# A hybrid block kernel on one core: every place of its side work set anew in its tables

## What is computed

```python
x = x + attn(_layernorm(x), ...)          # RMS norm, 16 heads, causal softmax, output projection, plus its own normed input
x = x + ffn(_layernorm(x), ...)           # base matrix + shared and 6 routed low-rank matrices, top 2
x = x + ssm(_layernorm(x), ...)           # conv of 4 taps, silu, softplus, scan with 16 states, gate, projection
x = x + ffn(_layernorm(x), ...)           # the same ffn once more

def step(h, inputs):                      # the scan of ssm, over the 512 rows
    dt, bt, ct, xt_ = inputs
    decay = jnp.exp(A[None] * dt[:, :, None])
    inp = dt[:, :, None] * xt_[:, :, None] * bt[:, None, :]
    h = decay * h + inp
    y = jnp.einsum('bdn,bn->bd', h, ct)
    return (h, y)
```

## Time and profile before

| | us |
|---|---|
| median of 3 runs | 1929.06 (1927.0 to 1930.86) |
| the profiled execution, its own time | 1925.6 |
| its span, first to last instruction | 1923.0 |
| PE busy | 1713.8 (89%) |
| DVE busy | 1676.4 (87%) |
| ACT busy | 1400.5 (73%) |
| POOL busy | 1102.4 (57%) |
| mean granted TensorE clock | 0.977 of 2.4 GHz |

### The profile page before, as it was taken

One profiled execution on the slowest core, in us unless ns is written; L12 is line 12 of the kernel. 1 busy time (PEld: TensorE's weight loads), 2 busy tenths in 40 slices (PEclk: granted clock), 3 DMA queues, 4 the chain that ended last, 5 costly groups with the idle time before them and its releaser, 6 DMA issues.

```text
span 1923.0 us, 31523 instructions
## 1 busy us (share of the span) xinstructions
PE 1713.8 (89%) x9575; PEld 1006.4 (52%) x9620; DVE 1676.4 (87%) x3928; ACT 1400.5 (73%) x2724; POOL 1102.4 (57%) x903
## 2 busy tenths in 40 slices
PE   6989797999989898999999898999999898878875
PEld 2555454646455564646465565646455464535333
DVE  4654889999999999999999999999999899977892
ACT  3666768787887978787887878787877868675541
POOL 2000575667666676657667666657667566666330
PEclk9999899999999999999999999999999999999997
DMA  5312576978879797988879797988889687661110
GB/s 142 90 56 78 127 170 138 182 157 178 154 158 182 159 181 150 183 156 179 157 164 178 158 185 151 180 155 179 152 169 170 150 169 147 137 127 49 56 60 11
DMA packets 216331, 275.30 MB, mean 143 GB/s; under 512 B 37170, under 2 KB 129123, under 8 KB 216163
## 3 DMA queue, kind: packets, MB, share of 16 engines
q0 software_dynamic: 60480, 110.13, 34.8%
q1 hardware_dynamic: 155682, 163.17, 33.4%
HBM read 128.49 MB, written 34.08 MB: 85 GB/s over the span
## 4 chain that ended last, share of the span: by engine, by line
PE 48%; DVE 15%; ACT 12%; issue 9%; DMA 8%; POOL 7%; SPq 1%; another core or an unknown queue 0%; POOLq 0%; DVEq 0%; ACTq 0%
PE bank L423 9%; DVE hc L1275 7%; PE bank L542 5%; PE bank L625 4%; DMA y<-hc 4%; PE bank L487 4%; PE bank L509 4%; PE bank L642 4%; POOL inp L1449 3%; PE bank L434 3%; DVE bank L1131 2%; PE bank L417 2%; ACT pt L916 2%; DVE hc L1283 2%; PE bank L626 2%
## 5 line engine op out<-in xcount | busy, mean ns | idle before, releaser
L1449 POOL TENSOR_TENSOR inp<-u,b_all 128x1024 f32<-128x1024 f32 x240 | 572.8, 2386 | 361.0 <-issue 125.0
L1275 DVE TENSOR_TENSOR_SCAN hc<-dec,inp 128x1024 f32<-128x1024 f32 x256 | 585.8, 2288 | 39.7 <-POOL inp L1449 15.2
L1131 DVE CUSTOM_DVE_ANT_0 bank<-bank,mask_qk 128x512 f32<-128x512 f32 (+3 forms) x1024 | 479.4, 509 | 85.6 <-PE bank L487 85.0
L1459 POOL DMA_DIRECT2D y<-hc x420 | 368.5, 949 | 129.5 <-DMA y<-hc 64.9
L916 ACT ACTIVATE pt<-bank 128x512 f32<-128x512 f32 x640 | 380.1, 605 | 72.5 <-PE bank L525 49.3
L1032 ACT ACTIVATE dec<-dt,a_neg 128x511 f32<-128x511 f32 x512 | 339.6, 729 | 34.1 <-DVE hc L1275 34.0
L1283 DVE TENSOR_TENSOR hc<-hc,bank 128x1024 f32<-128x1024 f32 x242 | 294.0, 1215 | 14.2 <-PE bank L679 13.3
L487 PE MATMUL bank<-sk,sq 96*128 96x512 bf16 (+3 forms) x1024 | 250.3, 306 | 27.3 <-DVE mall L1131 16.7
L509 PE MATMUL bank<-sq,sk 98*128 98x512 bf16 (+3 forms) x1024 | 248.6, 304 | 27.0 <-ACT pt L916 23.4
L542 PE MATMUL bank<-pt,v_sb 128*32 128x512 f32 (+3 forms) x2048 | 180.5, 450 | 7.5 <-ACT pt L916 6.8
L487 PEld LDWEIGHTS bank<-sk,sq 96*128 96x128 bf16 x1024 | 95.3, 99 | 145.0 <-issue 54.8
(11 more groups left out here) (169 smaller groups left out, 2999.0 us busy)
## 6 DMA issues: line engine op xcount, KB each, us to landing
y<-hc POOLq DMA_DIRECT2D x420, 256.0 KB, 4.9
b_all<-b_kept SPq DMA_DIRECT2D x256, 256.0 KB, 3.7
qk_parts<-parts SPq DMA_DIRECT2D x96, 256.0 KB, 3.0
sq<-qk_parts SPq DMA_DIRECT2D x384, 64.0 KB, 3.7
sk<-qk_parts SPq DMA_DIRECT2D x384, 64.0 KB, 3.9
X<-in_x SPq DMA_DIRECT2D x16, 512.0 KB, 6.1
out<-X SPq DMA_DIRECT2D x16, 512.0 KB, 3.3
sq<-hlt SPq DMA_DIRECT2D x256, 2.0 KB
```

The lines of the kernel that those rows point to most:

```text
L1131: return V.tensor_tensor_reduce(src[:, o:o + n], src[:, o:o + n], mask_qk[:, T - n:T], 1.0, -3.0e38, ALU.add, ALU.max, out)
L1275: V.tensor_tensor_scan(h, d, v, 0.0, ALU.mult, ALU.add).then_inc(scan_done.sem, 1)
L1449: G.tensor_tensor(inp[:, n % 2, :, :], u[:, :, :], b_all[:, k % 3, None, :].to_broadcast([P, C, T]), ALU.mult).then_inc(inp_ready.sem, 1)
L1459: pool.dma_start(y[:, s % 2, c, :], hc[:, (NS * s + n) % HC, c, :], accum_op=ALU.add).then_inc(y_added[c].sem, 16)
```

## The change

All five tables, those of the kinds 1 to 3 and `BANK` get other numbers. No instruction is added or removed, no wait is added or removed, and no code outside the tables changes. After the change the tables take one line less, so every line number of the code behind them is lower by one: line 487 becomes 486, and so on.

```diff
-    PE_AT = {"res": (-32, -29), "xn": (-73, -72), "qk00": (-56, -51, -47), "qk01": (-47, -44, -43),
+    PE_AT = {"res": (-32, -29), "xn": (-73, -72), "qk00": (-56, -50, -49), "qk01": (-47, -44, -43),
...
-    BANK = {"res": (0, 0), "xn": (0, 1), "qk00": 0, "qk01": 1, "v": (1, 1), "qk10": 0, "qk11": 1, "ao": (0, 1),
+    BANK = {"res": (0, 0), "xn": (1, 0), "qk00": 0, "qk01": 1, "v": (1, 1), "qk10": 0, "qk11": 1, "ao": (0, 1),
...
-    POOL_AT = {"rsqrt_f": 89, "rsqrt_s": 122, "rsqrt_q": -113, "rsqrt_l": 234, "low": (110, 258),
+    POOL_AT = {"rsqrt_f": 83, "rsqrt_s": 123, "rsqrt_q": -113, "rsqrt_l": 234, "low": (110, 258),
```

More of the change, by code:

```diff
@@ L121, in hybrid_block @@
-    SP_AT = {"parts": (-40, -3), "load_x": -114, "store_b": 149, "store": 280, "stack": (-32, -32, -33),
-             "maxima": -6, "load_b": (150, 151, 156, 160, 168, 173, 185, 185, 190, 198, 199, 210, 211, 215, 224, 225)}
+              "scan": (160, 167, 169, 171, 177, 185, 192, 197, 201, 205, 211, 214, 218, 224, 229, 232),
+              "product": (168, 170, 171, 177, 182, 190, 195, 199, 203, 210, 212, 215, 222, 227, 229, 236)}
+    POOL_AT = {"rsqrt_f": 83, "rsqrt_s": 123, "rsqrt_q": -113, "rsqrt_l": 234, "low": (110, 258),
+               "inputs": (147, 149, 152, 152, 157, 165, 175, 183, 191, 199, 206, 211, 214, 218, 220, 222),
+               "add": (160, 152, 159, 174, 176, 182, 187, 191, 200, 208, 212, 214, 219, 221, 223, 228)}
@@ L123, in hybrid_block @@
+    SP_AT = {"parts": (-40, -3), "load_x": -114, "store_b": 149, "store": 282, "stack": (-31, -31, -32),
+             "maxima": -10,
+             "load_b": (150, 152, 157, 160, 164, 172, 180, 187, 192, 198, 200, 209, 210, 213, 225, 225)}
     OWN = {
         1: {
[7 rows of a table removed]
-                   "sum": (136, 151, 160, 164, 165, 173, 174, 186, 189, 196, 202, 202, 218, 219, 225, 225)},
-            "ACT": {"res": (-51, -42), "square_f": 92, "square_s": 127, "norm_f": 98, "norm_q": -106, "norm_l": 254,
[4 rows of a table removed]
-                   "decays": (154, 157, 163, 167, 168, 180, 182, 190, 197, 202, 205, 210, 215, 219, 225, 228)},
@@ L139, in hybrid_block @@
[L139 to L145, removed]
@@ new lines, in hybrid_block @@
+            "ACT": {"res": (-53, -45), "square_f": 92, "square_s": 127, "norm_f": 98, "norm_q": -100, "exp0": 108,
[4 rows of a table added]
+                   "decays": (155, 155, 164, 166, 168, 180, 182, 189, 196, 204, 205, 211, 213, 217, 221, 226)},
+            "DVE": {"gated": 246, "add_x3": (248, 250), "in0": 109, "in1": 264, "out0": 112, "add_up1": (278, 278),
+                   "add_x1": (90, 90), "add_up0": (127, 129), "silu": 142, "delta": 152, "stats_q": -98,
+                   "scan": (160, 165, 166, 171, 180, 185, 192, 199, 201, 205, 211, 215, 217, 224, 227, 231),
+                   "product": (161, 165, 168, 179, 184, 187, 193, 200, 206, 209, 214, 215, 225, 229, 231, 238)},
@@ new lines, in hybrid_block @@
+            "POOL": {"rsqrt_f": 93, "rsqrt_s": 122, "rsqrt_q": -94, "rsqrt_l": 233, "low": (117, 260),
+                   "inputs": (137, 140, 153, 153, 157, 170, 172, 184, 196, 202, 205, 209, 210, 213, 215, 225),
+                   "add": (160, 156, 158, 171, 180, 180, 195, 197, 205, 206, 209, 212, 215, 225, 226, 228)},
+            "SP": {"parts": (-43, -10), "load_x": -103, "store_b": 152, "store": 286,
+                   "load_b": (152, 153, 157, 158, 169, 173, 181, 188, 189, 199, 199, 201, 216, 221, 225, 228)},
+        },
[8 rows of a table added]
+                   "sum": (167, 175, 180, 180, 185, 192, 198, 206, 210, 211, 215, 221, 224, 237, 241, 242)},
+            "ACT": {"res": (-30, -20), "square_f": 99, "square_l": 257, "norm_f": 102, "norm_s": 128, "norm_q": -101,
[4 rows of a table added]
+                   "decays": (152, 159, 164, 165, 171, 172, 177, 183, 196, 198, 202, 210, 212, 219, 222, 224)},
+            "DVE": {"gated": 240, "add_x3": (242, 246), "in1": 271, "out0": 116, "out1": 272, "add_up1": (288, 289),
+                   "add_x1": (95, 93), "add_up0": (124, 125), "silu": 139, "stats_q": -112,
+                   "scan": (158, 166, 169, 175, 183, 184, 190, 196, 200, 209, 214, 216, 216, 221, 225, 234),
+                   "product": (162, 170, 175, 176, 184, 184, 190, 198, 207, 209, 215, 220, 224, 224, 232, 235)},
+            "POOL": {"rsqrt_f": 89, "rsqrt_s": 121, "rsqrt_q": -106, "rsqrt_l": 249, "low": (110, 259),
+                   "inputs": (145, 149, 149, 149, 154, 166, 176, 195, 201, 202, 207, 208, 209, 213, 219, 219),
+                   "add": (160, 149, 151, 154, 171, 171, 182, 191, 201, 205, 205, 211, 215, 218, 220, 224)},
+            "SP": {"parts": (-39, 3), "store_b": 148, "store": 314,
+                   "load_b": (152, 153, 160, 162, 162, 180, 182, 186, 189, 189, 199, 202, 207, 208, 214, 219)},
+        },
[8 rows of a table added]
+                   "sum": (164, 169, 172, 175, 188, 196, 199, 204, 205, 213, 218, 225, 227, 228, 235, 240)},
+            "ACT": {"res": (-34, -30), "square_f": 95, "square_s": 119, "square_l": 243, "norm_f": 98, "norm_s": 123,
[4 rows of a table added]
+                   "decays": (146, 155, 159, 162, 169, 179, 180, 188, 193, 195, 201, 212, 218, 219, 220, 234)},
+            "DVE": {"gated": 241, "add_x3": (244, 253), "in1": 258, "out0": 114, "out1": 261, "add_up1": (273, 292),
+                   "add_x1": (95, 97), "add_up0": (122, 122), "silu": 137, "delta": 156, "stats_q": -112,
+                   "scan": (157, 159, 160, 169, 178, 186, 187, 202, 203, 204, 207, 209, 211, 221, 225, 228),
+                   "product": (158, 163, 173, 177, 183, 186, 193, 202, 203, 205, 208, 209, 214, 223, 226, 230)},
+            "POOL": {"rsqrt_f": 82, "rsqrt_s": 125, "rsqrt_q": -105, "rsqrt_l": 232, "low": (116, 247),
+                   "inputs": (140, 148, 149, 150, 155, 172, 175, 176, 184, 184, 194, 204, 212, 213, 215, 223),
+                   "add": (160, 155, 166, 176, 180, 187, 190, 194, 195, 216, 217, 217, 220, 220, 220, 229)},
+            "SP": {"parts": (-43, 2), "load_x": -112, "store_b": 141, "store": 289,
+                   "load_b": (164, 165, 165, 165, 165, 186, 188, 196, 197, 202, 203, 206, 219, 222, 226, 234)},
```

44 lines of the change are left out of this document (7 added, 37 removed), and 83 rows, old and new, of tables (ACT_AT, OWN, PE_AT).

## The result

The changed kernel takes **1910.06 us** (median of 4 runs, 1904.06 to 1914.16) against 1928.47 us for the kernel before in the same comparison: a ratio of 0.9897, 95% interval 0.9872 to 0.9921, 18.4 us less. Forecast were 1918.4 us, 10.7 less. The profiled execution is the slowest of the four, 1914.16 us.

What follows compares the result with a forecast made beforehand. Neither DVE nor PE alone was the bound: both nearly full, each held by the other or ACT. 0.37 + 0.2 + 0.5 = 1.07 us a frame, 10.7 for ten frames, gave 1918.4 us; range 1905 to 1931.

Steps and rivals of the forecast that it cites:

- A frame of 106.2 to 106.8 us: Sign of being right: time between convolutions in the changed kernel's middle, against 107.56 us before.
- if scans wait for inputs in the middle: Sign of being wrong: DVE's scans in middle frames wait for POOL's inputs; no size given.
- Place 1: PE between convolution and gate: exp ahead of drains, C's spreading behind score units; 0.37 us a frame, bounds 0 and 0.59.
- The decays: Part of Place 2: decays ahead of one cast on ACT end DVE's scan wait of 0.57 us.
- Place 2: PE and ACT after softplus: 0.57 us gained, 0.37 charged for DVE's new bank 2 wait; net 0.2 us a frame.
- Place 3: PE and POOL at tok_f's turning: turning fills PE's ot_sb wait, root ahead of inputs; 0.5 us a frame, bounds 0 and 0.85.
- The second rival: POOL's root ahead of the inputs makes DVE's scan late in middle frames; slower, 1941 us; chance 0.15.
- The first (waits only move): Rival: DVE's and PE's gains return as waits for each other; frame within 0.3 us of 107.56; chance 0.15.
- The third rival: More waits close than counted, the three places at upper bounds, 2.0 us a frame: 1909 us; chance 0.18.
- the rest ... together 0, bounds -4 and +4 us: Other middle moves and the tables for the first and last two batches: no net gain counted.
- if the gain comes from the start and the end: Sign of being wrong: the time is saved outside the middle frames; no size given.

Runs made afterwards that it cites:

- unit_back: The changed kernel with the score unit for bank 2 put back ahead of the matmuls into bank 7 in middle frames: 1910.07 us, 0.9904 of before.
- place3: The kernel before with only tok_f's turning and copies earlier and POOL's inverse root ahead of the inputs, in middle frames: ratio 1.0005.
- turn_y: The kernel before with only y turned by PE in one piece of eight instead of two of four, in middle frames: ratio 1.0002.
- named: The kernel before with the moves of Place 1, The decays, turn_y and place3, plus one number in the first batch's POOL table: ratio 0.9976.
- ends_new: The kernel before with the changed tables for the first and last two batches only, middle tables and BANK as before: ratio 1.0030.
- middle_new: The kernel before with the changed tables and BANK for the middle batches, old tables for the first and last two: ratio 1.0027.

## Why the prediction was right, and where it was off

- **"A frame of 106.2 to 106.8 us"**: right for three of the nine frames (106.6, 106.4, 106.8), wrong for their mean, 107.1; in `unit_back` five of nine lie there and the mean is 106.9. The middle was counted at 1.07 us a frame and gave 0.67 on average, 0.8 in `unit_back`. The sign **"if scans wait for inputs in the middle"** came true in four frames, by 5.2 us against 1.6 before; the prediction looked for it behind the root, and it came some 21 us behind the convolution. Place 1: 0.45 measured alone (0.37 counted). The decays: 0.57, as read from the wait.
- **Place 2's new wait**, "0.2 to 0.4 us": there, 0.35 us. But I charged it to the frame in full (-0.37), and taking it away brings 0.1 us. Place 2 as a whole is worth 0.57 - 0.1 = 0.47 us, not 0.2.
- **Place 3**: 0.5 us counted, 0.5 measured in one frame of the changed kernel, and 0 in the kernel before. The size was right, and the reason incomplete: I asked whether PE would be free and the rows normed, not whether DVE stood ahead of it.
- The sum of the three by these measurements is 0.45 + 0.47 + 0.5 = 1.4 us a frame; the frame at 921.90 gained 1.17. The other moves of the middle, counted at nothing, would then cost 0.2 to 0.3 us together, 0.1 of it the turning of y. That the sum of 1.07 came so close to this frame is in part luck: place 2 was counted too low, and these moves at nothing.
- **The second rival** (the root makes the scan late) did not come: the inputs behind it end 0.4 us before their scan, where the prediction had counted 0.3. In the earlier trace rows they ended 3.2 us before it. In `place3` the cover is all but used up: the inputs end at 993.87 and their scan begins at 993.96. The first (waits only move) is what `place3` and `turn_y` do alone, not the whole.
- **The third rival** (more waits close, 1909 us) is the one that 1910.06 us is nearest to, but not for its reason: it had the three places at their upper bounds, 2.0 us a frame.
- **The step that failed** most is the term "the rest ... together 0, bounds -4 and +4 us". Seven profiles have the tables of before for the first and last batches (apart from one number in `named`), five those of the change; these five have the changed tables in the middle too. Up to the third convolution they take 385.6 and 382.6 us on average, from the twelfth to the end 571.0 and 564.0. So start and end together bring 10 us, and the nine frames of the middle 6.0 in the profiled execution and 7.2 in `unit_back`'s. About 6 of them are shown to belong to the tables of the last batches: behind the thirteenth convolution the five take 455.2 to 458.1 us and the seven 460.7 to 465.6, and `ends_new` (455.5) and `middle_new` (465.2) fall on the side of their last tables. For the 3 us of the start this cannot be said. I had looked at the last 133 us alone and at the alternation of inputs and scan there, and held that no table shortens it. From the last convolution to the end it is 141.2 us instead of 143.6, 1.4 us less on average over the five and the seven. The larger part lies in the frames ahead of it, where work still overlaps: behind 1350 us DVE waits 5.9 us for score units instead of 10.9 (the kernel before first).

```profile
DVE bank L1131 <- PE bank L487: 10.9, 12, 2.7
DVE bank L1130 <- PE bank L486: 5.9, 6, 2.9
```

- The prediction also said that I am wrong "if the gain comes from the start and the end". Half of it does. That the forecast had the right sign and held the time in its range rests on the middle for 6 to 7 us; the rest I did not see. The middle alone would have given some 1921 us (1928.5 - 7, an estimate), near the forecast and still in the range. Which moves of the first and last tables bring it was not tried, beyond the one number in `named`.

Whether the mean of few profiles splits the 10 us well is uncertain to a few microseconds: the five stretches behind the twelfth convolution with the changed tables lie between 561.9 and 565.9 us, the seven with the old between 568.8 and 573.3. These do not overlap. The five starts with the changed tables lie between 379.1 and 386.4, the seven others between 384.5 and 386.8, and there the clock of the second frame weighs in.

## What to carry to other kernels

Where two full engines hold each other, walk down the one that is fuller (here DVE) and price each of its waits: in an undisturbed frame closing one gave back 0.45 of 0.66 us and 0.57 of 0.57, and two of them added up, while closing a wait of the other engine gave nothing, as it seems as long as the first still stood ahead of it. Count over many frames, not in the best one: here 1.17 us in one frame were 0.67 on average, since scans began to wait for inputs behind POOL's issues. A new wait is cheaper than its length if the next engine has slack behind it. And price start and end with the same waits view as the middle; tables tuned together can't be judged by transplanting one half, since one frame at the seam cost 8 to 9 us, and a table that has no kinds (here `BANK`) comes along unseen.

## What the runs showed of the hardware

TensorE's clock fell to its lower level (1.2 of 2.4 GHz) after waits of only 1.8 us, in 5 of 18 cases, and rarely after shorter ones (2 of 123 of 1.26 to 1.66 us, and twice with none over 1.25); the changed kernel's two such frames took 107.6 and 107.4 us, where their neighbours took 106.4 and 106.8. The Trainium skill, page "TensorE: Matmul & The Clock Gate", section "HAM oscillation — how this bites in real kernels", tells that a wait of PE for data can throw its clock back, so that the next work starts slow; its own case has waits of 3 to 5 us. The trace agrees in that the four matmuls behind such a wait took 3.15 us instead of 1.96, but here waits of 1.8 us were enough, and 13 of 18 had no such effect. The times of the changed kernel's four runs follow the mean granted clock: 1914.16 us at 0.973, 1911.82 and 1908.3 at 0.977, 1904.06 at 0.981.

A silu on DVE took 2.41 us in `unit_back` while POOL ran inputs beside it, where the same took 1.22 in the kernel before:

```profile
281.73 2.68 POOL L1448 TENSOR_TENSOR inp<-u,b_all 128x1024 f32<-128x1024 f32 x1
...
283.10 2.41 DVE L1237 SCALAR_TENSOR_TENSOR xc<-sp_t,xc 128x1024 f32<-128x1024 f32 x1
```

POOL's inputs end at 284.41 us and the silu at 285.51, 1.1 us later, so it looks as if the silu stood until they were over. It is the same pair of engines as in the earlier trace rows, here at the other one's cost.
